# One block of POOL's work moved: z of the last batch is made ahead of the scatter of the batch before it

## The chip, the core and the metric

The kernel runs on one core of a Trainium2 chip. The metric is the device time of one execution in microseconds. The core has five engines that each run their own list of instructions and wait for each other by semaphores: PE (matrix products), DVE (vector work), ACT (activations), POOL (vector work and indirect transfers) and SP, which here only issues transfers. Sixteen DMA engines carry them.

## The reference

Input are 16 sequences (batches) of 512 tokens with 256 features. Two blocks follow each other; each normalises its input, and its normalised output is added to x.

```
x = x + layernorm(attention(layernorm(x)))        # 16 heads, blocks of 64, a band and the end blocks
x = x + layernorm(ffn(layernorm(x)))
```

The ffn normalises once more, computes `abel_out = gelu(xn @ abel_w + abel_b)`, picks the best 2 of 8 experts for each token from `logits = xn @ moe_gate_w + moe_gate_b`, and adds their outputs, `gelu(xn @ ew1[e] + eb1[e]) @ ew2[e] + eb2[e]`, by the softmax of the two logits. The sum is multiplied by three matrices `expm(gens[i])`, mixed with `abel_out` by a sigmoid gate, and added to the ffn's input.

## The kernel before

The kernel has three parts: `front`, `experts` and `last`. `front` goes over the batches in steps s = 0 to 18, and in one step several batches are in flight: batch s is projected to q, k and v, batch s-1 attends, batch s-2 is finished (its context is normalised and added to x, which gives `x1`, and then z, the normalised input of the ffn), and batch s-3 is routed (z is transposed, the dense product with `abel_w` and the gate's weights gives `pre`, the best two experts and each token's place in an expert's list are found, and the rows of z are scattered to these places in `z_rows` in device memory). Steps 6 to 13 are a hardware loop over two steps; the others are written out, s being a plain number there. In steps 17 and 18 no batch attends any more. Batch 15, the last, is finished in step 17 and routed in step 18; batch 14 is routed in step 17.

What each engine does in a step is written out by hand, in a fixed order. The work around the change:

- POOL, in `step` behind `block.gpsimd`: third parts of the split q and k, `inverse` and `residual` of batch s-2 (L1386), `scatter` of batch s-3 (L1399: 8 indirect transfers, each of 128 rows of 265 numbers; while a batch attends they wait for marks of that work as well), and `normed` of batch s-2. `normed` waits for `g_ve`, takes a power of both variances (`rs`, L1406), waits for `g_mv1` and for the scatters that still read its buffer, copies `rstd1` (L1411) and makes z in four products (L1413). Two buffers `zb` alternate by batch: batch 15 and batch 13 use the same one.
- DVE: routes batch s-3 and gives its destinations (`to_row`, L1221, semaphore `g_dest`), then takes the statistics of `x1` of batch s-2 (`ve`, L1236 and L1237, then L1239).
- PE in step 18: `turn_z` of batch 15 (L785), then in this order the product of expert 4 (L832), the dense product of two of four token tiles (L796), expert 5, the other two tiles, expert 6, the ranks (L808 to L814), expert 7, the product for `eb2` (L901) and the total of the carry (L906). The expert products multiply `ew2` by the three rotation matrices; in the trace their source is `xnT` or `xn`, the two buffers into which SP loads `ew2` transposed, and `gA`.
- SP: loads `ew2` of expert 4 when the product of expert 2 is out, that of 5 behind 3, of 6 behind 4, of 7 behind 5 (L550). Ahead of expert 4's in step 17 stand loads of `ew1` for experts 0 to 3 (L558, `w` in the trace), behind expert 7's those for 4 to 7. Behind them come stores of `abel_rows` and `y_rows` of batch 14.
- At the end of `front` DVE makes a table of the expert tiles from the total (up to L1359), SP waits for it and writes 8 blocks of zero rows (L635), and when they have landed all engines pass on to `experts`. It goes over 72 tiles of 256 rows, loads them (L1536), applies the experts and adds the results to `y_rows`.

Of the kernel before, what the change touches and what calls it, by code (L numbers as in the profile page):

```python
# [142 lines left out]
def wait(eng, s, value):  # L143

    if not isinstance(value, int) or value > 0:
        eng.wait_ge(s, value)


def plain(eng):


    eng.nop(nofuse=True)  # L152
# [59 lines left out]
def front(nc, outer, a, z, kept, w1, w2, b1, b2):  # L212
# [3 lines left out]
    B, S, D, NTOK, KC, FC, RB = z.B, z.S, z.D, z.NTOK, z.KC, z.FC, z.RB  # L216
# [3 lines left out]
    with ctx:  # L220
# [177 lines left out]
        def steps(eng, step):  # L398


            for s in range(6):
                step(s, s % 2, s // 2)
            with eng.Fori(3, B // 2 - 1) as i:
                step(2 * i, 0, i)
                step(2 * i + 1, 1, i)
            for s in range(B - 2, B + 3):
                step(s, s % 2, s // 2)

        def here(s, lag):

            return not isinstance(s, int) or 0 <= s - lag < B
# [949 lines left out]
        @block.gpsimd  # L1361
        def _(pool):
            pool.wait_ge(s_rows, 1)

            def inverse(n, ready, per, var, mid, mid_sem, dst, dst_sem):

                pool.wait_ge(ready, per * n + per)
                plain(pool)
                nc.gpsimd.tensor_scalar(mid[:, :], var, EPS, None, ALU.add).then_inc(mid_sem, 1)
                pool.wait_ge(mid_sem, n + 1)  # L1370
                nc.gpsimd.tensor_tensor(dst[:, :], mid[:, :], kept.neg_half[:, :], ALU.pow).then_inc(dst_sem, 1)

            def ln1(b):
                inverse(b, s_stat, NTOK, mv[:, :, 1], veps, s_veps, rstd, s_rstd)

            def third_part(b, m):
                pool.wait_ge(s_part2, b * 4 + m + 1)
                nc.gpsimd.tensor_tensor(split[:, m, 2, :], resid[:, m % 2, :], split[:, m, 1, :],  # L1378
                                        ALU.subtract).then_inc(s_split, 1)

            def residual(b):
                pool.wait_ge(s_xr, (b + 1) * LOADS)
                plain(pool)
                for j in range(NTOK):
                    pool.wait_ge(s_cln, b * NTOK + j + 1)
                    nc.gpsimd.tensor_tensor(x1[:, j, :], x1[:, j, :], ctxn[:, j, :], ALU.add).then_inc(s_x1, 1)  # L1386

            def scatter(s, b, bp):
                pool.wait_ge(g_zw, b + 1)
                pool.wait_ge(g_zi, b + 1)  # L1390
                pool.wait_ge(g_dest, b + 1)
                plain(pool)
                for j in range(NTOK):
                    if j > 0 and (not isinstance(s, int) or s <= B):
                        pool.wait_ge(s_pv, (s - 1) * QUADS + SCATTER_AT[j])
                        plain(pool)
                    for k in range(TOPK):
                        idx = to_row[bp][:, j, k:k + 1]
                        pool.indirect_dma_start(kept.z_rows, bass.IndirectOffsetOnAxis(ap=idx, axis=0),  # L1399
                                                zb[bp][:, j, :], None).then_inc(g_scat[bp], 16)  # L1400

            def normed(b, bp, earlier):


                pool.wait_ge(g_ve, (b + 1) * 2)
                nc.gpsimd.tensor_tensor(rs[:, :, :], ve[:, :, :], neg_halves[:, :, :], ALU.pow).then_inc(g_rs, 1)  # L1406
                pool.wait_ge(g_rs, b + 1)
                pool.wait_ge(g_mv1, b + 1)
                wait(pool, g_scat[bp], earlier * SCATTERS)
                plain(pool)  # L1410
                nc.gpsimd.tensor_copy(kept.rstd1[:, bass.ds(b * NTOK, NTOK)], rs[:, 0, :])  # L1411
                for j in range(NTOK):
                    nc.gpsimd.tensor_scalar(zb[bp][:, j, 0:D], x1[:, j, :], mv0[:, j, 0:1], rs[:, 1, j:j + 1],  # L1413
                                            ALU.subtract, ALU.mult).then_inc(g_z, 1)

            def step(s, par, i):
                if here(s, 0):
                    for m in range(4):
                        third_part(s, m)
                if not isinstance(s, int) or s + 1 < B:  # L1420
                    ln1(s + 1)
                if here(s, 2):
                    b = s - 2
                    inverse(b, s_cstat, NTOK, cmv[:, :, 1], cveps, s_cveps, crstd, s_crstd)
                    residual(b)
                if here(s, 3):
                    scatter(s, s - 3, 1 - par)
                if here(s, 2):
                    normed(s - 2, par, i - 1)

            ln1(0)
            pool.wait_ge(g_init, N_INIT)
            steps(pool, step)
            for i in range(2):
                pool.wait_ge(g_scat[i], (B // 2) * SCATTERS)
# [541 lines left out]
```

## Time and profile before

| | |
|---|---|
| time before, median of 3 runs | 1994.57 us (1987.76 to 1997.65) |
| profiled execution, its own time | 2002.51 us |
| its span | 2000.7 us |
| PE busy | 1591.1 us, 80% |
| DVE busy | 1223.5 us, 61% |
| ACT busy | 928.4 us, 46% |
| POOL busy | 707.2 us, 35% |

Busy times are those of the profiled execution. The share of an engine is an average over stages that have different limits, so the stages must be read one by one. Times of instructions are given in us from the start of the span.

### The profile page before, as it was taken

How to read it: one execution, taken by the hardware profiler on the slowest of the kernel's cores; microseconds unless marked ns; L12 is line 12 of the kernel's file. 1: busy time of each engine (PE TensorE's matmuls, PEld its weight loads, DVE VectorE, ACT ScalarE, POOL GpSimd, SP SyncE). 2: the span in 40 equal slices, each digit the busy share in tenths (PEclk: the TensorE clock that was granted, in tenths of full speed). 3: DMA queues.
4: the chain of work that ended last, by engine and by line, in shares of the span. 5: the costliest groups of instructions: out<-in, count | busy, mean ns of one | idle time of the engine just before them, and what ended most of it. 6: DMA issues, size and time to landing. Idle time of an engine off the chain costs nothing. (4 is left out here: it accounts for less than half of the span.)

```text
span 2000.7 us, 35686 instructions
## 1 busy us (share of the span) xinstructions
PE 1591.1 (80%) x10365; PEld 1075.6 (54%) x10430; DVE 1223.5 (61%) x3633; ACT 928.4 (46%) x1788; POOL 707.2 (35%) x716
## 2 busy tenths in 40 slices
PE   3878888887887887887888887747999999999800
PEld 2534444444444444444444444536888888888700
DVE  6746765765765765765756755333565656565367
ACT  1045655655655655655656657412333333333234
POOL 1011223413413413314324313432445444444457
PEclk9889999999999998999999999978999999999955
DMA  3453256256265355364365351564665665566477
GB/s 118 78 107 83 55 124 134 82 126 144 72 127 118 89 137 112 81 146 105 90 148 101 82 138 66 167 204 104 139 137 97 142 135 113 123 135 119 49 257 253
DMA packets 185576, 241.78 MB, mean 121 GB/s; under 512 B 24584, under 2 KB 156048, under 8 KB 185296
## 3 DMA queue, kind: packets, MB, share of 16 engines
q1 hardware_dynamic: 158544, 203.58, 40.2%
q0 software_dynamic: 26880, 36.33, 10.9%
q8 instruction: 76, 1.25, 0.3%
q14 instruction: 76, 0.62, 0.1%
HBM read 133.40 MB, written 105.91 MB: 120 GB/s over the span
## 5 line engine op out<-in xcount | busy, mean ns | idle before, releaser
L956 ACT ACTIVATE pexp<-scT 128x512 f32<-128x512 f32 x768 | 440.6, 599 | 366.0 <-PE scT L743 323.7
L1126 DVE TENSOR_REDUCE mx<-work 128x1 f32<-128x320 f32 (+2 forms) x1024 | 493.3, 549 | 60.1 <-PE work L723 57.8
L1600 POOL DMA_INDIRECT y_rows<-rows_add,row_of x144 | 227.0, 1576 | 294.6 <-DMA y_rows<-rows_add,row_of 210.0
L723 PE MATMUL work<-w 126*128 126x320 bf16 (+4 forms) x1280 | 268.0, 302 | 60.3 <-DVE mx L1126 26.6
L743 PE MATMUL scT<-w 128*128 128x192 bf16 (+3 forms) x1472 | 258.8, 274 | 62.8 <-ACT pexp L956 56.9
L1632 PE MATMUL h_ps<-inT,w1c 128*128 128x256 f32 x1152 | 262.1, 381 | 2.4 <-DVE inT L1684 2.4
L1645 PE MATMUL o_ps<-w,hT 128*128 x1152 | 260.4, 379 | 0.0
L1632 PEld LDWEIGHTS h_ps<-inT,w1c 128*128 128x128 f32 x1152 | 219.7, 191 | 33.1 <-issue 3.1
L743 PEld LDWEIGHTS scT<-w 128*128 128x128 bf16 x1536 | 125.6, 98 | 205.4 <-ACT pexp L956 141.6
L1575 ACT ACTIVATE rows_add<-rows_out,row_share 128x257 f32<-128x257 f32 x144 | 65.6, 503 | 355.2 <-DVE rows_out L1700 256.5
L1645 PEld LDWEIGHTS o_ps<-w,hT 128*128 128x128 f32 x1152 | 213.4, 190 | 26.1
L1399 POOL DMA_INDIRECT z_rows<-z,to_row x128 | 125.6, 981 | 239.3 <-DVE to_row L1221 118.4
L723 PEld LDWEIGHTS work<-w 126*128 126x128 bf16 x1280 | 110.4, 98 | 162.1 <-DVE mx L1126 78.0
L1378 POOL TENSOR_TENSOR split<-resid,split 128x512 bf16<-128x512 f32 x64 | 73.5, 1158 | 248.9 <-ACT split L928 248.9
L1693 DVE TENSOR_TENSOR rows_out<-o_ps,b 128x512 f32<-128x512 f32 x72 | 49.9, 693 | 158.6 <-PE o_ps L1645 158.6
L700 PE MATMUL work<-xnT,wqkv 128*128 128x512 f32 x256 | 131.2, 662 | 10.1 <-issue 9.4
L1386 POOL TENSOR_TENSOR x<-x,ctxn 128x256 f32<-128x256 f32 x64 | 46.5, 728 | 245.2 <-ACT ctxn L947 245.2
L1567 ACT ACTIVATE hT<-h_ps,b1c 128x256 f32<-128x256 f32 x288 | 112.3, 463 | 38.0 <-PE h_ps L1632 38.0
L1110 DVE SCALAR_TENSOR_TENSOR resid<-work,bqk_sb,split 128x512 f32<-128x512 f32 x64 | 47.7, 750 | 109.2 <-ACT split L923 89.8
L1137 DVE RECIPROCAL rden<-turn 128x16 f32<-128x16 f32 x64 | 15.8, 247 | 151.4 <-PE turn L775 151.4
L760 PE MATMUL pv<-pexp,vaug 128*32 128x192 f32 (+3 forms) x1536 | 105.4, 393 | 1.2 <-ACT pexp L956 0.9
L760 PE MATMUL pv<-pexp,b 128*32 128x192 f32 (+3 forms) x1536 | 104.7, 392 | 0.0
(173 smaller groups left out, 2172.2 us busy)
## 6 DMA issues: line engine op xcount, KB each, us to landing
w<-split_spill SPq DMA_DIRECT2D x384, 128.0 KB, 5.9
split_spill<-split SPq DMA_DIRECT2D x64, 384.0 KB, 4.7
rows_in<-z_rows SPq DMA_DIRECT2D x72, 265.0 KB, 4.7
y_rows<-pre SPq DMA_DIRECT2D x16, 514.0 KB, 6.6
y<-y_rows SPq DMA_DIRECT2D x16, 514.0 KB, 6.1
x_rows<-x SPq DMA_DIRECT2D x16, 512.0 KB, 2.7
abel_rows<-pre SPq DMA_DIRECT2D x16, 512.0 KB, 5.5
abel_in<-abel_rows SPq DMA_DIRECT2D x16, 512.0 KB, 4.5
```

What stands on the lines that cost most here:

```text
L700: ins = nc.tensor.matmul(work[w][:, :], wqkv[:, k, col:col + P], xnT[:, k, :], start=(k == 0), stop=(k == KC - 1))
L723: ins = nc.tensor.matmul(work[t][:, at:at + hi - lo], tile(qst[par][0:K_SCORE, h, :], t), kst[par][0:K_SCORE, h, lo:hi], start=True, stop= ...
L743: ins = nc.tensor.matmul(scT[n % 2][:, at:at + hi - lo], tile(kst[par][0:K_EXP, h, :], t), qst[par][0:K_EXP, h, lo:hi], start=True, stop=True)
L760: ins = nc.tensor.matmul(pv[32 * n:32 * n + 32, lo:hi], vaug[par][:, t, h, :], pexp[:, (q * GROUP + n) % NPB, at:at + hi - lo], start=(c = ...
L956: nc.scalar.activation(pexp[:, (q * GROUP + n) % NPB, :], scT[n % 2][:, :], ACT.Exp, scale=DH ** -0.5).then_inc(s_exp, 1)
L1126: nc.vector.reduce_max(mx[:, c:c + 1], work[t][:, 0:n], AX_X).then_inc(w_free[t], 1)
L1378: nc.gpsimd.tensor_tensor(split[:, m, 2, :], resid[:, m % 2, :], split[:, m, 1, :], ALU.subtract).then_inc(s_split, 1)
L1399: pool.indirect_dma_start(kept.z_rows, bass.IndirectOffsetOnAxis(ap=idx, axis=0), zb[bp][:, j, :], None).then_inc(g_scat[bp], 16)
L1567: nc.scalar.activation(hT[par][:, f, :], h_ps[par][:, f * RT:(f + 1) * RT], ACT.Gelu, bias=b1c[par][:, f:f + 1]).then_inc(e_hT, 1)
L1600: pool.indirect_dma_start(kept.y_rows, bass.IndirectOffsetOnAxis(ap=row_of[n][:, r:r + 1], axis=0), rows_add[n % 2][:, r, :], None, comput ...
L1632: ins = nc.tensor.matmul(h_ps[par][:, f * RT:(f + 1) * RT], w1c[par][:, k, f * P:(f + 1) * P], inT[par][:, k, :], start=(k == 0), stop=(k ...
L1645: ins = nc.tensor.matmul(o_ps[par][:, r * D:(r + 1) * D], hT[par][:, f, r * P:(r + 1) * P], w2[:, bass.ds(e, 1), f, :].rearrange("p o d -> ...
```

## The change

In the written-out steps behind the attention (s over 16) POOL calls `normed` before `scatter`; in all other steps the order stays.

```diff
@@ -1423,9 +1423,12 @@
                     b = s - 2
                     inverse(b, s_cstat, NTOK, cmv[:, :, 1], cveps, s_cveps, crstd, s_crstd)
                     residual(b)
+
+                if isinstance(s, int) and s > B and here(s, 2):
+                    normed(s - 2, par, i - 1)
                 if here(s, 3):
                     scatter(s, s - 3, 1 - par)
-                if here(s, 2):
+                if here(s, 2) and (not isinstance(s, int) or s <= B):
                     normed(s - 2, par, i - 1)
```

This is POOL's list before, from the residual of batch 15 in step 17 (the first two rows) to the end of `front`. The first two rows of L1399 are the scatter of batch 14, the last two that of batch 15.

```order
L1386 TENSOR_TENSOR x<-x,ctxn 128x256 [waits s_xr,s_cln]
L1386 TENSOR_TENSOR x<-x,ctxn 128x256 [waits s_cln] x3
L1399 DMA z_rows<-z,to_row 67840x265 [waits g_dest,g_zw,g_zi]
L1399 DMA z_rows<-z,to_row 67840x265 x7
L1406 TENSOR_TENSOR rs<-ve,neg_halves 128x8 [waits g_ve]
L1411 COPY rstd<-rs 128x4 [waits g_scat1,g_rs,g_mv1]
L1413 TENSOR_SCALAR z<-x,mv,rs 128x256 x4
L1399 DMA z_rows<-z,to_row 67840x265 [waits g_dest,g_zw,g_zi]
L1399 DMA z_rows<-z,to_row 67840x265 x7
L220 UNCONDITIONAL_BRANCH [waits g_scat1,g_scat0]
```

And this is the same place of the changed kernel:

```order
L1386 TENSOR_TENSOR x<-x,ctxn 128x256 [waits s_xr,s_cln]
L1386 TENSOR_TENSOR x<-x,ctxn 128x256 [waits s_cln] x3
L1406 TENSOR_TENSOR rs<-ve,neg_halves 128x8 [waits g_ve]
L1411 COPY rstd<-rs 128x4 [waits g_scat1,g_rs,g_mv1]
L1413 TENSOR_SCALAR z<-x,mv,rs 128x256 x4
L1399 DMA z_rows<-z,to_row 67840x265 [waits g_dest,g_zw,g_zi]
L1399 DMA z_rows<-z,to_row 67840x265 x7
L1399 DMA z_rows<-z,to_row 67840x265 [waits g_dest,g_zw,g_zi]
L1399 DMA z_rows<-z,to_row 67840x265 x7
L220 UNCONDITIONAL_BRANCH [waits g_scat1,g_scat0]
```

The three rows that make z of batch 15 have moved ahead of the eight transfers of batch 14. Everything before and behind is as it was, and the lists of PE, ACT, DVE and SP are the same in both kernels. On PE, where the transposes of step 18 wait for that z (`g_z`), the list reads so in both; the first row is the last product of expert 3 in step 17, rows with `xnT` or `xn` are those of experts 4 and 5:

```order
L832 MATMUL work<-gA,xn 128x256 x3
L785 MATMUL work<-ident_sb,z 128x128 [waits g_z,w_free0]
L785 MATMUL work<-ident_sb,z 128x128 [waits g_z] x3
L785 MATMUL work<-ident_sb,z 128x128 [waits g_z,w_free1]
L785 MATMUL work<-ident_sb,z 128x128 [waits g_z] x3
L832 MATMUL work<-gA,xnT 128x256 [waits w_free2,r_w20]
L832 MATMUL work<-gA,xnT 128x256 x3
L832 MATMUL work<-gA,xnT 128x256 [waits w_free3]
L832 MATMUL work<-gA,xnT 128x256 x3
L796 MATMUL work<-wab,zT 128x265 [waits w_free0,w_free1]
```

Nothing moved here. `r_w20` is the semaphore of the load of `ew2` for even experts.

## Rows read from the trace of the kernel before

**Rows 1.** Busy time by stage: us, PE, PEld, DVE, ACT, POOL, PEclk, DMA share, GB/s

```profile
1331.60:1357.20 25.60, 0.00 (x0) 0.00 (x0) 10.14 (x44) 0.65 (x2) 5.87 (x7) 0.56 0.71 215
1357.20:1870.00 512.80, 507.75 (x2479) 446.44 (x2480) 296.34 (x991) 162.15 (x410) 231.61 (x204) 0.99 0.58 122
```

**Rows 2.** Timeline of SP's issues: start, us, line, operation, out<-in, count

```profile
1288.55 3.74 SPq L558 DMA_DIRECT2D w<-in_ew  x4
1292.34 0.47 SPq L550 DMA_DIRECT2D xnT<-in_ew2T  x1
...
1344.26 8.44 SPq L635 DMA_DIRECT2D z_rows<-pexp  x8
1357.22 3.83 SPq L1536 DMA_DIRECT2D rows_in<-z_rows  x4
```

**Rows 3.** Timeline of DVE, statistics of batch 15 and the table's end

```profile
1290.85 0.16 DVE L1237 TENSOR_SCALAR ve<-mv 128x4 f32<-128x4 f32 x1
...
1343.04 0.20 DVE L1359 CAST table<-pexp 128x72 int32<-128x72 f32 x1
```

**Rows 4.** Timeline of PE in steps 17 and 18; in brackets: idle before and releaser

```profile
1288.43 3.62 PE L832 MATMUL work<-gA,xn 128*128 128x256 f32 x16
1304.66 0.45 PE L785 MATMUL work<-ident_sb,z 128*128 128x128 f32 x1 [12.62 <-POOL z L1413]
...
1308.19 1.33 PE L785 MATMUL work<-ident_sb,z 128*128 128x128 f32 x5 [0.72 <-POOL z L1413]
1309.31 5.98 PE L832 MATMUL work<-gA,xnT 128*128 128x256 f32 x16
...
1316.92 3.61 PE L832 MATMUL work<-gA,xn 128*128 128x256 f32 x16
...
1322.21 3.62 PE L832 MATMUL work<-gA,xnT 128*128 128x256 f32 x16
...
1331.31 0.18 PE L906 MATMUL work<-carry,ones 128*128 128x8 bf16 x1
```

**Rows 5.** Timeline of POOL in steps 17 and 18

```profile
1289.47 1.11 POOL L1399 DMA_INDIRECT z_rows<-z,to_row  x1 [1.39 <-DVE to_row L1221]
...
1301.26 1.69 POOL L1406 TENSOR_TENSOR rs<-ve,neg_halves 128x8 f32<-128x8 f32 x1
...
1303.29 4.84 POOL L1413 TENSOR_SCALAR z<-x,mv,rs 128x256 f32<-128x256 f32 x4
1329.34 1.10 POOL L1399 DMA_INDIRECT z_rows<-z,to_row  x1 [21.21 <-DVE to_row L1221]
```

**Rows 6.** DMA issues at 1292.3, 1294.3, 1315.3: KB, us to landing; software queue, 1268 to 1360

```profile
xnT<-in_ew2T SPq DMA_DIRECT2D x1, 512.0 KB, 9.7
...
y_rows<-pre SPq DMA_DIRECT2D x1, 514.0 KB, 14.2
...
xnT<-in_ew2T SPq DMA_DIRECT2D x1, 512.0 KB, 3.5
...
q0 software_dynamic: 768, 2.17, 7.3%
```

**Rows 7.** Windows while the loads land, columns as in the first group

```profile
1292.00:1297.00 5.00, 0.05 (x1) 0.00 (x0) 0.00 (x0) 1.55 (x2) 3.42 (x4) 1.00 0.89 293
1297.00:1302.00 5.00, 0.00 (x0) 0.00 (x0) 0.00 (x0) 0.00 (x0) 4.07 (x5) 0.50 1.04 404
```

**Rows 8.** Windows around two falls of PE's clock, same columns

```profile
400.00:401.00 1.00, 0.00 (x0) 0.00 (x0) 0.00 (x0) 0.99 (x2) 0.00 (x0) 1.00 0.91 217
401.00:402.00 1.00, 0.53 (x3) 0.48 (x4) 0.00 (x0) 1.00 (x3) 0.00 (x0) 1.00 1.13 156
...
403.00:404.00 1.00, 0.74 (x5) 0.18 (x3) 0.00 (x0) 0.94 (x2) 0.00 (x0) 0.50 1.16 141
...
1297.00:1297.50 0.50, 0.00 (x0) 0.00 (x0) 0.00 (x0) 0.00 (x0) 0.45 (x1) 0.52 1.08 401
...
1314.00:1314.50 0.50, 0.50 (x4) 0.45 (x3) 0.00 (x0) 0.00 (x0) 0.00 (x0) 0.91 0.00 0
```

## The prediction

> **What bounds the kernel now.** I read the stages first [rows 1]. From 1357.2 on PE is busy 507.75 of 512.80 us, so the expert stage passes on every microsecond by which it starts earlier, and the last stage hangs behind it. Ahead of it lies a stretch of 25.6 us in which PE does nothing at all. So the question is what sets the end of the attention part, and I followed it back from SP [rows 2]: the first load of the expert stage goes out at 1357.22, behind the eight stores of zero rows that begin at 1344.26. These wait for DVE's table, whose last instruction starts at 1343.04 [rows 3]. The table is a chain of small DVE instructions behind PE's total of the carry, at 1331.31 [rows 4]. PE itself works nearly without a gap from 1308.19 to 1331.49: the last transposes of z of batch 15, the product with `ew2` of expert 4 (e=4 below) at 1309.31, half of the dense product, e=5 at 1316.92, the other half, e=6 at 1322.21, the ranks, e=7, the total. Before 1308.19 PE is idle but for three single transposes (the first at 1304.66), from the end of e=3 (1288.43 + 3.62 = 1292.05). It waits for z of batch 15, and POOL [rows 5] has not made it: POOL scatters batch 14 from 1289.47, and only at 1301.26 begins z (1.69 for the power, 4.84 for the four products, done at 1308.13). The values that z needs were there long before: DVE's second `ve` starts at 1290.85 and takes 0.16 [rows 3].
>
> So the path to the end is: POOL's scatter of batch 14, z of batch 15, PE's step 18, the table, the zero rows, the experts.
>
> **The change part by part.** Nothing is removed or added. The test holds for steps written out with s over 16, which are 17 and 18; in step 18 there is no z left to make. So one group of three rows on POOL moves ahead of one group of eight scatters, once. The other four engines have the same instructions and the same waits.
>
> *z of batch 15.* POOL can begin once DVE's `ve` and the copy behind it are done, at 1291.1 where it was 1301.26. The wait that z adds on the scatters of its own buffer concerns batch 13, long done. Its duration stays 6.9, so z is done at 1298.0 and not at 1308.13. First term: 10.1 us.
>
> *PE's transposes.* They follow z as now: 1309.3 less 10.1 is 1299.2 for the end of the last.
>
> *e=4, the next in PE's order,* stands ahead of the dense product and needs its half megabyte of `ew2` beside z. Now that is no wait. But SP issues that load at 1292.34 behind four loads of `ew1` that begin at 1288.55 [rows 2], and it takes 9.7 us [rows 6]: it lands at 1302.0, later than 1299.2. If nothing else changed, the gain would shrink here to 1309.3 - 1302.0 = 7.3 us. Something does change: the eight scatters now go out after 1298.0. Sixteen of them move 2.17 MB [rows 6], so one moves 0.136 MB, and about five have been written by 1302. That is 0.68 MB, at the 404 GB/s of 1297 to 1302 [rows 7] 1.7 us: the load lands at 1300.3. With 293 GB/s from 1292 to 1297 the engines were not at their best rate while POOL was scattering, and the four SP issues took 3.74, where the one behind them took 0.47; both may get better, and then the load is down by about 1299 and PE's transposes decide again. Between 1299.2 and 1300.3 I take 1299.8. Second term: 10.1 becomes 9.5.
>
> The Trainium skill (DMA: Bandwidth & Descriptors, "Anatomy of one DMA") fits a transfer as 2.0 us and its bytes at 436 GB/s. The trace's lone 512 KB load takes 3.5 [rows 6], the fit gives 3.2. By the fit, an estimate from that page alone, the backlog of 3.15 MB ahead of and with this load, from 1288.2 on, would be down at 1297.4; the second term would then vanish and the sum would be 10.1. The trace at 293 and 404 GB/s does not bear out such a rate for this mix, and I stay with 9.5.
>
> *The clock.* The granted clock fell to half at 1297.0, 4.9 us after PE's last work, and rose at 1314.0, 5.8 us after steady work began [rows 8]. e=4 ran in this dip: 5.98 for 16 matmuls, against 3.62 at full clock [rows 4]. After the change PE is still idle from 1292.05 to about 1294.4, then does three transposes of 0.45, one per 1.2 us, five in a row, and waits for the load. Is this enough to keep the clock? Elsewhere it fell with more work than that: PE was busy 0.00 and 0.53 us in the two microseconds from 400 on, and at half clock in 403 [rows 8]. So I expect the dip again, and e=4 in it again. Its length is not fixed: at best e=4 runs at full clock (2.4 gained), at worst all of it at half (16 matmuls at twice 3.62, 7.2; 1.3 lost). Third term: 0, from +2.4 to -1.3.
>
> *The eight scatters behind z.* Now they take 11.8, from 1289.47 to 1301.26 [rows 5]; behind z they run from 1298.0 to 1309.8 at the latest. Behind them on POOL stands only the scatter of batch 15, which waits for DVE until 1329.34 now and until 1319.8 then: hidden, with 10 us to spare. Were the cover gone, each microsecond of overlap would move the last scatters by as much, and these, 11.8 from 1329.34, end at 1341.1 now, 16 us ahead of the expert stage. But their bytes now fall behind 1298. There SP issues the load for e=6 when e=4 is done, at 1299.8 + 6.0 = 1305.8. In the idle queue of now it took 3.5 [rows 6]. e=6 starts 12.9 after e=4 [rows 4], at 1312.7, so the load may take 6.9. The backlog in front is gone by about 1306, since the bytes are the same as now, when the engines fell idle at 1308; three scatters remain. I take 5 us: hidden. The load for e=7 comes later still.
>
> *The tail.* DVE's table, the spill of `eb2`, the zero rows all hang on PE's end or on DVE; each shifts with it. Cost 0.
>
> Sum: 10.1 - 0.6 + 0 = 9.5 us.
>
> **How the numbers follow.** The profiled execution took 2002.51 us for a span of 2000.7, 7.9 above the median of 1994.57. Less 9.5 it gives 1993.0, and 1985.1 for the median. A measurement of this kernel tells a change from none at about 0.5%, 10.0 us, so the forecast is a gain of 0.48% just under that line.
>
> **The rivals.**
> - *The clock stays up* (15%). z comes 10.1 earlier, PE's unbroken idle stretch is cut from 12.6 us to 2.4, and e=4 takes 3.62. For it: PE's gap is shorter than the 4.9 after which the clock fell. Against it: the dip at 402. Gain 9.5 + 2.4 = 11.9, time 1982.7. The Trainium skill (TensorE: Matmul & The Clock Gate, "What's actually happening") holds that the throttled state is the default and activity lifts it; both the fall and the rise in this trace agree, but neither settles which way this thin work goes.
> - *The load for e=4 gets nothing from the missing scatters* (12%). It lands at 1302.0 or later, gain 7.3, time 1987.3.
> - *The load for e=6 becomes the wait* (10%). It shares the engines with the scatters. If it took the 9.7 us that e=4's took in the backlog, it would land at 1315.5, 2.8 late: gain 6.7. With the 14.2 of the y rows [rows 6] it would be 1320.0, 7.3 late: gain 2.2, time 1992.4.
> - *Slower* (4%). The same mechanism taken further: the e=6 load would have to be later than e=6 starts now, 1322.21, that is over 16.4 us under way. From there on it is a loss, beyond 0.5% only from 26 us on. The longest that any transfer of this stretch took is 14.2. At 27 us the time would be 2005.
> - *The change does nothing* (4%): something else than z opens PE's step 18, as a late bank or DVE. The trace names POOL's z for all of these waits, so this needs an error in the records.
>
> My forecast itself has 55%: a gain of 8 to 11 us. The runs shown spread from 1987.76 to 1997.65 and a median of three moves by some 3 us. Taking in the bounds of the terms (7.3 - 1.3 = 6.0 and 12.5), half of the e=6 case and this spread, the range is 1978 to 1993. Faster by over 0.5%: nearly half of the forecast's 55, most of the kept clock's 15, little of the rest: 0.42. Slower: 0.04. Same: 0.54.
>
> **What would show it.** In the changed trace POOL's power for z starts at 1291 and its first scatter of batch 14 at 1298. PE's single transposes start near 1294.5 and e=4 at 1299.2 to 1300.3; if later, the load's landing will name the reason. The 16 matmuls of e=4 take 6 us with the dip, 3.6 without. From e=5 to the experts' first load the distance is 1357.22 - 1316.92 = 40.3 as before. The first load goes out near 1347.7. The prediction is wrong if this load moves by 9.5 and the time doesn't (then the experts don't pass it on), if e=6 waits for its load, or if e=4 starts after 1302.

## The result and the profile after

The changed kernel takes 1986.82 us (median of 15 executions), the kernel before 1997.65 beside it; the ratio is 0.9946, with a 95% interval of 0.9932 to 0.9960, a gain of 10.8 us. One of the 15 executions took 8898.21 us, far out of line with all others, and is left out of the ratio. The forecast was a gain of 9.5 us or 0.48%, just under the line of 0.5%; the interval of the gain, 0.40 to 0.68%, lies across that line, so on which side of it the gain falls is not settled. The changed kernel was timed twice more beside the experiments: 0.9952 (0.9927 to 0.9976) and 0.9946 (0.9930 to 0.9963).

POOL's timeline of the changed kernel in steps 17 and 18, to be laid beside [rows 5]:

```profile
1280.12 1.65 POOL L1406 TENSOR_TENSOR rs<-ve,neg_halves 128x8 f32<-128x8 f32 x1 [3.01 <-DVE ve L1237]
1281.92 0.19 POOL L1411 COPY rstd<-rs 128x4 f32<-128x4 f32 x1 [0.16 <-POOL rs L1406]
1282.09 4.83 POOL L1413 TENSOR_SCALAR z<-x,mv,rs 128x256 f32<-128x256 f32 x4
1287.10 1.11 POOL L1399 DMA_INDIRECT z_rows<-z,to_row  x1 [0.17 <-issue]
...
1309.14 0.95 POOL L1399 DMA_INDIRECT z_rows<-z,to_row  x1 [12.07 <-DVE to_row L1221]
```

The power now waits for DVE's `ve` and for nothing else. The scatter of batch 14 stands behind z, and POOL still waits 12 us for the destinations of batch 15. By the distance from the start of the product of expert 3 (1277.44, below) z is done at 9.5 us, where 9.6 was forecast, and the eight scatters end at 19.6.

PE of the changed kernel, beside [rows 4]:

```profile
1277.44 3.62 PE L832 MATMUL work<-gA,xn 128*128 128x256 f32 x16
1283.46 0.45 PE L785 MATMUL work<-ident_sb,z 128*128 128x128 f32 x1 [2.41 <-POOL z L1413]
...
1286.98 1.33 PE L785 MATMUL work<-ident_sb,z 128*128 128x128 f32 x5 [0.72 <-POOL z L1413]
1289.26 5.85 PE L832 MATMUL work<-gA,xnT 128*128 128x256 f32 x16 [0.95 <-DMA xnT<-in_ew2T]
...
1296.74 3.62 PE L832 MATMUL work<-gA,xn 128*128 128x256 f32 x16
...
1302.03 3.62 PE L832 MATMUL work<-gA,xnT 128*128 128x256 f32 x16
...
1311.13 0.18 PE L906 MATMUL work<-carry,ones 128*128 128x8 bf16 x1
```

The unbroken wait for z is 2.41 us where it was 12.62. The product of expert 4 (e=4) waited 0.95 for its load and ran at the lower level of the granted clock for most of its time again (a clock dip).

SP of the changed kernel, beside [rows 2]:

```profile
1277.58 3.00 SPq L558 DMA_DIRECT2D w<-in_ew  x4
1280.62 0.84 SPq L550 DMA_DIRECT2D xnT<-in_ew2T  x1
...
1295.14 0.37 SPq L550 DMA_DIRECT2D xnT<-in_ew2T  x1
...
1323.92 8.36 SPq L635 DMA_DIRECT2D z_rows<-pexp  x8
1336.34 3.82 SPq L1539 DMA_DIRECT2D rows_in<-z_rows  x4
```

The loads of `ew2` for e=4 (issued at 1280.62) and e=6 (issued at 1295.14); the last column is us to landing:

```profile
xnT<-in_ew2T SPq DMA_DIRECT2D x1, 512.0 KB, 8.6
...
xnT<-in_ew2T SPq DMA_DIRECT2D x1, 512.0 KB, 4.5
```

Absolute times can't be compared between two profiles here: the product of expert 3 (e=3), ahead of which both kernels do the same, starts at 1288.43 in one profile and at 1277.44 in the other. Over the twelve profiles of this study it lies between 1275.78 and 1291.79. So the table below counts every time from the start of that product. "Total" is PE's total of the carry, "zero rows" and "first load" are when SP begins to issue them. "Rest" is the span less the first load of the expert stage.

| kernel | POOL begins z | e=4 starts | e=4 takes | e=5 | e=6 | total | zero rows | first load | rest |
|---|---|---|---|---|---|---|---|---|---|
| before | 12.83 | 20.88 | 5.98 | 28.49 | 33.78 | 42.88 | 55.83 | 68.79 | 643.5 |
| changed | 2.68 | 11.82 | 5.85 | 19.30 | 24.59 | 33.69 | 46.48 | 58.90 | 646.0 |
| changed, 2nd profile | 2.67 | 10.84 | 5.97 | 18.43 | 23.73 | 32.83 | 45.61 | 58.20 | 643.1 |
| changed, 3rd profile | 2.67 | 10.91 | 5.59 | 18.13 | 23.42 | 32.52 | 45.32 | 58.01 | 641.9 |
| half of the scatter ahead | 7.80 | 15.84 | 5.46 | 22.93 | 28.22 | 37.32 | 50.10 | 64.11 | 643.9 |
| scatter held back | 2.67 | 10.87 | 5.61 | 18.10 | 23.39 | 32.50 | 45.30 | 63.82 | 644.6 |
| load of e=4 first | 2.68 | 10.67 | 5.15 | 17.45 | 23.30 | 32.51 | 45.28 | 58.57 | 642.3 |
| PE kept at work | 2.67 | 10.81 | 3.72 | 16.16 | 21.45 | 30.55 | 43.33 | 57.49 | 649.0 |
| both of these | 2.68 | 10.16 | 3.62 | 15.41 | 20.70 | 29.80 | 42.61 | 54.82 | 643.1 |
| z on DVE | 2.67 | 6.50 | 3.62 | 13.41 | 22.07 | 32.96 | 45.75 | 58.08 | 645.2 |
| z first in all steps | 2.67 | 11.66 | 6.32 | 19.61 | 24.90 | 34.00 | 46.80 | 58.77 | 643.8 |
| z on DVE, loads spread | 2.68 | 6.98 | 4.82 | 13.42 | 18.72 | 27.82 | 40.60 | 53.80 | 644.1 |

The first load comes 9.9, 10.6 and 10.8 us earlier in the three profiles of the changed kernel, which is the gain that the timings show. In the rest no effect of the change can be seen: it varies by some us with no order in it.

### The profile page after: what moved, and what is told of

The parts are those of the page before. It is cut to its first block and busy times, and to the rows that moved or that the text cites. A ratio compares the mean times of both kernels' runs of the same rounds, so it can differ in the third digit from the quotient of the medians.

```text
span 1982.3 us, 35750 instructions
## 1 busy us (share of the span) xinstructions
PE 1587.0 (80%) x10429; PEld 1070.9 (54%) x10430; DVE 1222.7 (62%) x3633; ACT 928.3 (47%) x1788; POOL 707.9 (36%) x716
## 5 line engine op out<-in xcount | busy, mean ns | idle before, releaser
L743 PE MATMUL scT<-w 128*128 128x192 bf16 (+3 forms) x1536 | 274.4, 277 | 55.0 <-ACT pexp L956 54.3
L1399 POOL DMA_INDIRECT z_rows<-z,to_row x128 | 125.4, 980 | 227.1 <-DVE to_row L1221 107.9
L700 PE MATMUL work<-xnT,wqkv 128*128 128x512 f32 x256 | 124.0, 631 | 9.6 <-issue 8.9
```

The source lines that it names most:

```text
L700: ins = nc.tensor.matmul(work[w][:, :], wqkv[:, k, col:col + P], xnT[:, k, :], start=(k == 0), stop=(k == KC - 1))
L743: ins = nc.tensor.matmul(scT[n % 2][:, at:at + hi - lo], tile(kst[par][0:K_EXP, h, :], t), qst[par][0:K_EXP, h, lo:hi], start=True, stop=True)
```

## The experiments

All are edits of the changed kernel. The excerpts show the main lines of each edit, not all; in the first, `scatter` also takes the token tiles as an argument. The kernels were timed in three groups, each beside the kernel before on its chip.

**Half of the scatter ahead of z.**

```diff
-                    normed(s - 2, par, i - 1)
-                if here(s, 3):
-                    scatter(s, s - 3, 1 - par)
+                if s_is(s, B + 1):
+                    scatter(s, s - 3, 1 - par, range(0, 2))
+                    normed(s - 2, par, i - 1)
+                    scatter(s, s - 3, 1 - par, range(2, NTOK))
```

> Two of the four token tiles of batch 14 are scattered ahead of z of batch 15, two behind it. Measure: from the start of expert 3's product on PE to the first load of the expert stage, 68.8 us in the kernel before and 58.9 in the changed one. If POOL's z sets when PE's step 18 begins, four scatters (about 5.1 us at 1.27 each, less the 1.6 by which the first could start ahead of DVE's statistics) come back: z starts 3.5 to 5 us later than in the changed kernel, the distance is 62 to 64 us and the time lies half way, near 1992. If instead the gain came from keeping scatters away from the loads of expert weights, the distance follows the landing of these loads and not z. If the gain was noise of the front, the distance is between neither.

Measured: 0.9991 (0.9974 to 1.0008) of the kernel before. POOL's timeline of this kernel:

```profile
1289.12 0.98 POOL L1399 DMA_INDIRECT z_rows<-z,to_row  x1 [2.08 <-issue]
...
1291.68 0.97 POOL L1399 DMA_INDIRECT z_rows<-z,to_row  x1 [0.30 <-issue]
1292.67 1.68 POOL L1406 TENSOR_TENSOR rs<-ve,neg_halves 128x8 f32<-128x8 f32 x1
```

Four scatters ahead of z put it 5.1 us later than in the changed kernel, and e=4 starts 4.0 to 5.0 later: half the dose, about half the effect up to PE's total (37.32, between 32.5 to 33.7 and 42.88). The load for e=4 shows the dose too. It landed 13.6 us behind the start of e=3 with all eight scatters ahead of z, 12.4 with four, and 10.8 to 11.8 with none. The first load lies at 64.11, at the far edge of what was expected, because the zero rows took 14.0 from the first issue to the first load instead of 12.4 to 12.7. By that distance the kernel should be 4.7 us, 0.24%, faster than the one before; the interval of the timing just includes it and also includes no gain, and it does not reach the expected half way, near 0.997. So half the effect is shown by the trace alone.

**The scatter of batch 14 held back to the end.**

```diff
+                if s_is(s, B + 2):
+                    pool.wait_ge(g_dest, B)
+                    scatter(s, s - 4, par)
-                if here(s, 3):
+                if here(s, 3) and not s_is(s, B + 1):
                     scatter(s, s - 3, 1 - par)
```

> On top of the change the scatter of batch 14 is held back until the destinations of batch 15 are there, so that 16 scatters run back to back at the end of the attention part and none runs beside the loads of experts 4 to 6. If the scatters behind z are hidden and cost nothing, the start of expert 4's product moves by at most 1 us (the wait of 0.95 for its load may go, if the scatters were its reason, which I doubt since they start only 0.2 us after z), and the distance from expert 3's product to the first load of the expert stage stays within 1 us of 58.9: 16 scatters of 1.27 from 1309 end near 1329.4 plus some 4 to 6 to land, just ahead of 1336. If the scatters do delay the loads, expert 4 or 6 starts earlier and the distance falls by up to 2. If POOL's end matters, it rises by a few us.

Measured: 0.9986 (0.9971 to 1.0001). The first half of the expectation held: e=4 starts at 10.87, as in the second and third profile of the changed kernel (10.84, 10.91), and the total lies at 32.50. So the scatters behind z cost PE nothing at e=4. At e=6 they cost its load 1 us, which is hidden: it takes 3.5 without them here, as in the kernel before, and 4.3 to 4.5 in the changed one. The second half was wrong. The first load moved by 5 to 6 us, from between 58.0 and 58.9 to 63.82. POOL's timeline of this kernel:

```profile
1318.77 1.11 POOL L1399 DMA_INDIRECT z_rows<-z,to_row  x1 [20.97 <-DVE to_row L1221]
...
1339.71 0.96 POOL L1399 DMA_INDIRECT z_rows<-z,to_row  x1 [0.30 <-issue]
```

SP's timeline of it:

```profile
1333.61 9.17 SPq L635 DMA_DIRECT2D z_rows<-pexp  x8
1352.13 3.82 SPq L1542 DMA_DIRECT2D rows_in<-z_rows  x4
```

and the longest wait of SP in that stretch, followed by that of the changed kernel:

```profile
SPq L220 <- DMA z_rows<-pexp: 7.8, 1, 7.8
...
SPq L220 <- DMA z_rows<-pexp: 2.5, 1, 2.5
```

The 16 scatters end at 1340.67. The expected 1329.4 was counted in the first profile of the changed kernel, where expert 3 starts 10.9 us earlier; 1340.3 in this one, so their number and pace were right. What I had not priced is that they now share the engines with SP's eight stores of zero rows, whose last lands late: SP waits 7.8 us for it, 2.9 in the kernel before and 2.5 in the changed one. From the first issue of the zero rows to just behind the start of the next stage the engines moved 4.00 MB at 206 GB/s on average here, and 2.69 MB at 205 GB/s in the changed kernel: the rate is the same and the bytes are more. What is left of the gain, 5.0 us or 0.25%, lies inside the interval of the timing. The scatter of batch 14 is hidden where the change puts it, and not beside the zero rows, the last 12 us ahead of the expert stage.

**The load of expert 4 ahead of those of `ew1`.**

```diff
                     sp.wait_ge(s_sc, B * UNITS)
-                    load_w1(range(NE // 2))
                     load_w2_behind(4)
+                    load_w1(range(NE // 2))
```

> On top of the change SP issues the load for expert 4 ahead of the four loads of ew1 instead of behind them. My theory: in the changed kernel expert 4's product waited 0.95 us for this load behind the transposes, so the wait vanishes, expert 4 starts where the transposes end, and the distance from expert 3's product to the first load of the expert stage falls from 58.9 to about 58.0; the time by as much, too little for the timing. Rival: the half clock or the copies of z behind the transposes hold the product anyway and nothing moves.

Measured: 0.9963 (0.9944 to 0.9981). PE's timeline of this kernel:

```profile
1293.20 1.33 PE L785 MATMUL work<-ident_sb,z 128*128 128x128 f32 x5 [0.72 <-POOL z L1413]
1294.32 5.15 PE L832 MATMUL work<-gA,xnT 128*128 128x256 f32 x16
...
1306.95 3.72 PE L832 MATMUL work<-gA,xnT 128*128 128x256 f32 x16 [0.40 <-DMA xnT<-in_ew2T]
```

e=4 follows the transposes without a wait. It starts at 10.67. In the second and third profile of the unaltered changed kernel it starts at 10.84 and 10.91, with no wait that the trace names, but the load lands at 10.8 in both. So this order brings the 0.2 to 1.2 us by which the load comes behind the transposes. And e=6 now waits 0.40, which it did not before: its load, issued 0.7 to 1.9 us earlier, took 7.4 us instead of 4.3 to 4.5. Why it took longer isn't shown; issued 2 us earlier still it took 5.5 (both edits together, below).

**PE kept at work while it waits for z.**

```diff
                 for j in range(NTOK):
+                    if s_is(s, B + 2) and k == 0:
+                        for n in range(3 if j == 0 else 1):
+                            cols = S if j == 0 else D
+                            nc.tensor.matmul(pv[:, 0:cols], ident_sb[:, :], wqkv[:, 0, 0:cols], start=True, stop=True)
                     pe.wait_ge(g_z, b * NTOK + j + 1)
```

> On top of the change PE runs six matrix products nobody reads, three of 128x512 while it waits for the first piece of z in step 18 and one of 128x256 ahead of each further piece, into the bank of the attention's output, free by then. They add nothing to the result. Theory: the clock falls because PE has too little work here; with it the clock stays at full, the transposes and expert 4's product run at 3.6 us instead of 5.85, and the distance from expert 3's product to the first load of the expert stage falls from 58.9 by 2 to 2.5 us (the wait for the load grows by what the transposes gain, 0.5). Rival: the fall does not depend on this work; then expert 4 still takes near 6 us and the distance stays or rises a little.

Measured: 0.9958 (0.9942 to 0.9975). PE's timeline of this kernel:

```profile
1298.26 0.77 PE L789 MATMUL work<-ident_sb,z 128*128 128x128 f32 x5 [0.44 <-POOL z L1417]
1299.53 3.72 PE L836 MATMUL work<-gA,xnT 128*128 128x256 f32 x16 [0.50 <-DMA xnT<-in_ew2T]
```

The windows of the changed kernel at the same place (us, PE, PEld, DVE, ACT, POOL, granted clock, DMA share, GB/s), for [rows 8]:

```profile
1283.00:1284.00 1.00, 0.45 (x1) 0.18 (x1) 0.00 (x0) 0.00 (x0) 1.00 (x2) 0.68 0.91 262
1284.00:1285.00 1.00, 0.42 (x1) 0.18 (x1) 0.00 (x0) 0.00 (x0) 1.00 (x2) 0.50 0.95 313
...
1292.00:1293.00 1.00, 1.00 (x4) 0.82 (x3) 0.00 (x0) 0.00 (x0) 0.70 (x2) 0.50 1.03 230
1293.00:1294.00 1.00, 1.00 (x5) 0.84 (x4) 0.00 (x0) 0.58 (x1) 0.70 (x2) 0.70 1.00 275
```

and those of the kernel with PE kept at work:

```profile
1295.00:1296.00 1.00, 0.59 (x4) 0.19 (x3) 0.00 (x0) 0.00 (x0) 1.00 (x2) 1.00 1.05 391
1296.00:1297.00 1.00, 0.62 (x3) 0.22 (x2) 0.00 (x0) 0.00 (x0) 1.00 (x2) 1.00 1.03 391
```

Three products of 128x512 ahead of the first piece of z and one of 128x256 ahead of each further piece hold the clock at its upper level; the last five transposes take 0.77 instead of 1.33, e=4 3.72 instead of 5.6 to 6.0, and PE's total comes 2 to 3 us earlier. At the first load 0.5 to 1.4 of that is left, since in this profile the zero rows took 14.2 us. The dip came in all six profiles in which POOL makes z ahead of the whole scatter and PE does nothing but the transposes, and in neither of the two with the added products. So it is a consequence of what PE does between e=3 and e=4, the gap and the thin work behind it together. Its price is 2.0 to 2.3 us at PE's total, against the two profiles in which e=4 hardly waited for its load. When the clock falls differs: the mean of 0.68 in the row from 1283 on puts the fall at 1283.4, 2.3 us behind PE's last work (1281.06) and ahead of the first transpose; in the second profile it fell 5.0 us behind e=3, after three transposes had begun. The timing can't tell this kernel from the changed one.

**Both together.** The edits are those two.

> Both additions together: the load for expert 4 ahead of those of ew1, and PE kept at work with products that nobody reads. With the load early, expert 4 starts where the transposes end, 9.8 us behind expert 3's start plus 0.5 (10.2), against 10.8 with either alone. With the clock up it takes 3.6. Then expert 6's product, 13 us behind, is at risk: its load waited 0.40 in the run with the load order alone, where it was issued 15.9 us behind expert 3. Here it is issued at 13.9 behind, into the same backlog, so it lands near 22.5 and is wanted at 20.9: a wait of about 1.5. PE's total then lies 31 to 32 us behind expert 3, no better than with the products alone (30.55). If the backlog doesn't bind, it lies at 30.0.

Measured: 0.9951 (0.9929 to 0.9973). e=4 starts at 10.16, as expected, and e=6 at 20.70 without a wait: the feared backlog did not bind. The total lies at 29.80 and the first load at 54.82, 3.2 to 4.1 us ahead of those of the three profiles of the changed kernel. In time it stands beside 0.9952 for the changed kernel of the same group: 3 to 4 us, 0.2%, are below what the timing resolves.

**The changed kernel again.**

> The changed kernel itself once more, as a measure for the three beside it and for the four of the call before. If the first ratio of 0.9946 was the true size, it comes back between 0.993 and 0.996; the kernels with two more edits that share all of the change gave 0.9963 and 0.9958, so I expect 0.9952. In the trace: expert 3's product to the first load of the expert stage 58.9 us, give or take 1, and both clock and load as in the first profile of it: expert 4's product near 5.9 us, waiting up to 1 us for its load.

Measured: 0.9952 (0.9927 to 0.9976); the table (2nd profile) has what its trace shows: first load at 58.20, e=4 in 5.97 us. The trace names no wait for the load here.

**z of batch 15 on DVE**, with the load order of above.

```diff
                     if finish and q == STATS_AT:
                         second_stats(s - 2)
+                        if s_is(s, B + 1):
+                            dve.wait_ge(g_rs, B)
+                            dve.wait_ge(g_scat[par], (i - 1) * SCATTERS)
+                            plain(dve)
+                            for j in range(NTOK):
+                                nc.vector.tensor_scalar(zb[par][:, j, 0:D], x1[:, j, :], mv0[:, j, 0:1],
+                                                        rs[:, 1, j:j + 1], ALU.subtract, ALU.mult).then_inc(g_z, 1)
...
                 for j in range(NTOK):
+                    if isinstance(b, int) and b == B - 1:
+                        continue
```

The second part leaves POOL's four products out for the last batch.

> On top of the change and the early load, DVE makes z of batch 15 from POOL's power, in four products of 128x256 at some 0.41 us instead of 1.21; the arithmetic is the same. z is done 3.2 us earlier (1.6 against 4.84), the transposes end near 7.5 us behind expert 3 instead of 10.3. If z still sets the start, expert 4 starts 7.5 us behind expert 3 instead of 10.67 and the total lies 3 us earlier, less what the load for expert 6 takes back. If a load or the clock takes over, the gain is under 1.5 us and the wait stands at expert 4 or 6 with the DMA as its releaser.

Measured: 0.9964 (0.9942 to 0.9985). PE's timeline of this kernel:

```profile
1296.81 1.64 PE L785 MATMUL work<-ident_sb,z 128*128 128x128 f32 x8 [1.40 <-DVE z L1305]
1298.29 3.62 PE L832 MATMUL work<-gA,xnT 128*128 128x256 f32 x16
...
1305.20 3.72 PE L832 MATMUL work<-gA,xn 128*128 128x256 f32 x16 [1.51 <-DMA xn<-in_ew2T]
...
1313.86 5.41 PE L832 MATMUL work<-gA,xnT 128*128 128x256 f32 x16 [3.10 <-DMA xnT<-in_ew2T]
```

DVE's products:

```profile
1296.25 1.38 DVE L1305 TENSOR_SCALAR z<-x,mv,rs 128x256 f32<-128x256 f32 x4 [1.79 <-POOL rs L1413]
```

and the load for e=6, issued at 1301.93:

```profile
xnT<-in_ew2T SPq DMA_DIRECT2D x1, 512.0 KB, 11.9
```

z sets the start here too: e=4 starts at 6.50, 4.2 us earlier than with the load order alone. But the whole 4.2 is taken back: PE's total lies at 32.96, against 32.51. e=5 waits 1.51 for its load, e=6 3.10 for one that took 11.9 us, and the clock fell 0.8 us into e=6, behind that wait (the granted clock is 1.00 up to 1314.0 and 0.81 on average in the microsecond from there), so e=6 ran 5.41. This is the rival of the prediction, "the load for e=6 becomes the wait", come true once e=4 starts 4.2 us earlier still and its load is issued 10.1 us behind the start of e=3 instead of 15.9.

**The same with the loads spread.** Beside DVE making z as above, the edit is

```diff
-                    load_w1(range(NE // 2))
                     load_w2_behind(4)
+                    load_w1(range(0, 2))
                     load_w2_behind(5)
                 if s_is(s, B + 2):
                     load_w2_behind(6)
+                    load_w1(range(2, 3))
                     load_w2_behind(7)
-                    load_w1(range(NE // 2, NE))
+                    load_w1(range(3, NE))
```

> DVE makes z as in the run before, and SP's loads of ew1 are spread: two behind the load for expert 4, one behind that for expert 6, the other five behind that for expert 7. In that run PE waited 1.51 us for the load for expert 5 and 3.10 for expert 6's, which took 11.9 us behind four loads of ew1 and two stores, and the clock fell in the wait. If the backlog is the reason, both waits go, expert 6 starts near 17 to 18 us behind expert 3 instead of 22.07 and runs at 3.6, the total lies at 26 to 28 instead of 32.96 and the first load of the expert stage at 52 to 54 instead of 58.1; more loads behind expert 7's may cost 1 to 2 of it at the end, where the spill of eb2 queues behind them. The time is then 0.992 of the kernel before. If something else held expert 6, the wait stays.

Measured: 0.9932 (0.9911 to 0.9954), and in the same group the changed kernel:

> The changed kernel beside it on the same chip: ratio 0.995, the first load of the expert stage 58.2 to 58.9 us behind expert 3's product.

0.9946 (0.9930 to 0.9963), first load at 58.01. PE's timeline with the loads spread:

```profile
1291.72 2.16 PE L786 MATMUL work<-ident_sb,z 128*128 128x128 f32 x8 [1.40 <-DVE z L1306]
1293.68 4.82 PE L833 MATMUL work<-gA,xnT 128*128 128x256 f32 x16
...
1300.12 3.62 PE L833 MATMUL work<-gA,xn 128*128 128x256 f32 x16
...
1305.42 3.62 PE L833 MATMUL work<-gA,xnT 128*128 128x256 f32 x16
```

Both waits for loads are gone; e=6 starts at 18.72 instead of 22.07, at full clock, and its load took 6.0 us:

```profile
xnT<-in_ew2T SPq DMA_DIRECT2D x1, 512.0 KB, 6.0
```

A dip came in e=4, which the run before, with the same gap of 1.40 us ahead of the transposes, did not have. It makes e=6 0.7 later than expected and had its load issued 1.7 us later than in the run before, which may have helped the load as well. The first load lies at 53.80, 4 to 5 us ahead of the changed kernel's. It has the lowest ratio of all (0.992 was expected), but its interval overlaps with that of the changed kernel beside it. That it is faster than the changed kernel is shown in the trace up to the first load, not in the time.

**z first in every step.**

```diff
-                if isinstance(s, int) and s > B and here(s, 2):
+                if here(s, 2):
                     normed(s - 2, par, i - 1)
                 if here(s, 3):
                     scatter(s, s - 3, 1 - par)
-                if here(s, 2) and (not isinstance(s, int) or s <= B):
-                    normed(s - 2, par, i - 1)
```

> z ahead of the scatter in every step, the loop too. In a step with attention the scatter is spread over the step by waits on PE's progress and z of the newest batch is wanted only in the next step, so an earlier z brings nothing there, and in these steps the statistics that z waits for are taken late, at quad 8 of 12, behind the destinations at quad 6: POOL would stand still from about the end of the residual until then and start the scatter later, 5 to 10 us, with its next step's third parts of q and k and the norm of the next batch behind it. If POOL's slack covers that, the time is that of the changed kernel within 0.2%. If it doesn't, 13 steps pay some us each and the time is 10 to 60 us above it.

Measured: 0.9970 (0.9950 to 0.9991), the changed kernel of the same group 0.9952 (0.9927 to 0.9976). POOL's timeline of this kernel in a step with attention:

```profile
1132.11 1.65 POOL L1406 TENSOR_TENSOR rs<-ve,neg_halves 128x8 f32<-128x8 f32 x1 [14.46 <-DVE ve L1237]
...
1139.14 1.12 POOL L1399 DMA_INDIRECT z_rows<-z,to_row  x1 [0.18 <-issue]
...
1148.18 0.96 POOL L1399 DMA_INDIRECT z_rows<-z,to_row  x1 [0.30 <-issue]
1150.97 1.16 POOL L1378 TENSOR_TENSOR split<-resid,split 128x512 bf16<-128x512 f32 x1 [1.83 <-ACT split L928]
```

and of the kernel before in the same step:

```profile
1122.48 1.11 POOL L1399 DMA_INDIRECT z_rows<-z,to_row  x1 [6.12 <-DVE to_row L1221]
...
1137.97 1.68 POOL L1406 TENSOR_TENSOR rs<-ve,neg_halves 128x8 f32<-128x8 f32 x1
...
1149.71 1.16 POOL L1378 TENSOR_TENSOR split<-resid,split 128x512 bf16<-128x512 f32 x1 [4.85 <-ACT split L928]
```

POOL stands still for 14.46 us until DVE's statistics, and its scatter starts late, but the split behind waits for ACT in both kernels; POOL's slack ahead of it shrinks from 4.85 to 1.83 us. Both profiles are 1.26 to 1.28 us apart at the start and at the end of this step, so it takes equally long. That holds for the other steps as well, at equal granted clock: counted from POOL's `crstd` of one step to that of the next, the loop's steps take by turns 70.5 us where the clock is 1.00 and 71.7 to 71.8 where it is 0.98, and 79.5 to 79.9 us at 0.98, 80.9 to 81.0 at 0.96 and 82.7 to 82.8 at 0.94, in this kernel as in those with the order unchanged. The time is 0.18% above that of the changed kernel of the group, as expected within 0.2%, and the intervals overlap. In the steps with attention the order is free as long as this slack lasts. The change had to be made only where no attention hides POOL.

## Why the prediction was right, point by point

- *z of batch 15, 10.1 us earlier.* From 12.83 to 2.68: 10.15. POOL waits for `ve` alone. The half dose moved it by half. The rival "the change does nothing" falls with it.
- *Second term, 0.6 lost to the load of e=4.* The forecast had the load land between 1299.2 and 1300.3, 10.8 to 11.9 us behind the start of e=3, where it landed at 13.6 before. It landed at 11.8, 10.8 and 10.8, and e=4 started 9.06, 10.04 and 9.97 us earlier than before. Against the 10.15 of z the term was 1.1 in one profile and 0.1 to 0.2 in the two others; the kernel with z first in every step, the same here, waited 0.77. Both reasons given for the earlier landing came in: SP issued the load at 2.6 to 3.2 instead of 3.9, and it took 7.8 to 8.6 us instead of 9.7. That the scatters are the reason of the second is borne out by the other runs: with four of them ahead it took 9.8 us, and 7.0 to 8.6 in the six profiles with none ahead and the order of the loads unchanged. The reading of [rows 7] behind it was weak, though: POOL scattered in both windows, that of 293 and that of 404 GB/s. The run with the scatter held back started e=4 at 10.87, so the scatters behind z are not what makes the load late at times; what does stays open.
- *The clock, 0.* It fell again, and e=4 took 5.85, 5.97 and 5.59 against 5.98. The rival "the clock stays up" fell; what it would have given is shown by the run that kept PE at work, 2.0 to 2.3 us at PE's total (2.4 was forecast). The reason given for it, a gap shorter than the 4.9 us after which the clock fell before, does not hold: in the first profile it fell 2.3 us behind PE's last work.
- *The scatters behind z, hidden.* The load for e=6 was issued at 1295.14 and took 4.5 us (5 was taken) with no wait at e=6. The run on DVE shows where the rival begins: issued 10.1 us behind the start of e=3 instead of 17.7, in a kernel that also has the load of e=4 first, the same load takes 11.9 and takes all back.
- *The tail, 0.* From e=5 to the first load 39.6, 39.8 and 39.9, against 40.3: it gave 0.4 to 0.7 more. The zero rows make most of it, 12.4 to 12.7 against 13.0. In other runs this leg took 11.97 to 14.2 with no scatter beside it; what sets that is not settled.
- *Sum.* 9.5 was forecast. 9.9 to 10.8 came out in the traces at the first load, and 10.8 (8.0 to 13.6) in time. The 0.4 to 1.3 us more than forecast come from three places, each under a microsecond: the start of e=4 (-0.4 to +0.5), the stretch from there to e=5 (0 to 0.4) and the tail (0.4 to 0.7). In the first profile a loss at the load and a gain in the tail cancel, so that its 9.9 lies so near 9.5 is in part luck. That the expert stage passes it on is borne out by the rest, 641.9 to 646.0 against 643.5. The forecast time, 1985.1, is near the measured 1986.82 with the kernel before at 1997.65 instead of 1994.57 beside it, so the gains are to be compared and not the times.
- *The absolute mark* "first load near 1347.7" was a bad one: 1336.34 was measured, 11.0 of which come from a front that happened to run faster up to expert 3. It should have been given as a distance.

The Trainium skill's fit (DMA: Bandwidth & Descriptors, "Anatomy of one DMA") is given there for transfers that GpSimd issues, and this load is SP's. The estimate from it put the landing at 1297.4, 9.0 us behind the start of e=3. The trace does not agree: the load landed at 10.8 to 11.8. Only what would have followed, that it is no wait, came within 0.2 us of the truth in two of the three profiles.

## What to carry to other kernels

Where a pipeline drains, look at each engine's order again: an order that the steady state hides (the steps take equally long there either way) can put one engine's housekeeping straight on the path when the cover is gone. When several transfers and a product compete behind such a wait, removing the wait brings the next one close; here the first ten microseconds came from one moved block alone, and the next three to five, up to the first load, took two or more further edits (the load order with PE kept at work, or z on DVE with the loads spread). Compare profiles by distances from a mark ahead of the change, not by absolute times.

## What was not expected of the hardware

- Up to expert 3's product the same instructions took between 1275.8 and 1291.8 us in twelve profiles, one of them with a different order in the loop. That is 0.8% of the span and more than the change itself. In the loop the difference comes in portions of 1.2 to 1.8 us for a whole step and goes with the granted clock of that step (70.5 us at 1.00 and 71.8 at 0.98, as above). What makes the clock dip in one profile and not in another isn't shown.
- Eight stores of 265 KB of zero rows behind one another took 12.0 to 14.2 us until the next stage began, and 18.5 beside scatters.
- DVE's multiply and subtract for z took 1.38 us for four instructions of 128x256 where POOL took 4.84.
